# A post-norm decoder layer on one core: the order of steps on five engines, and which PSUM bank each step uses

## What is computed

```python
x = layernorm(x + self_attn(x, Wqkv, q_norm_w, k_norm_w, Wo))   # 16 heads of 32, RMS norm, RoPE, window 256 >= 128 tokens
x = layernorm(x + xattn(x, ctx, ctx))    # q, k, v taken as [8 heads, 16, 512]: scores are 512 x 512 per head, softmax, times v
x = layernorm(x + quant_dequant(x) @ quant_dequant(weight).T)   # blocks of 128, float8_e4m3
```

## Time and profile before

| | before |
|---|---|
| three timed runs, us | 3165.31, 3169.12, 3169.35 (median 3169.12) |
| the profiled execution, us | 3158.94, span 3157.2 |
| mean granted TensorE clock | 0.991 |
| PE busy | 2997.6 us, 95% of the span |
| DVE / ACT / POOL busy | 77% / 65% / 55% |

### The profile page before, as it was taken

How to read it: one execution, slowest core, us unless ns; L and a number is a source line. 1 busy time by engine, 2 the same in 40 slices (tenths; PEclk the granted TensorE clock), 3 DMA queues, 4 the chain that set the end, 5 groups by cost and what they waited for, 6 DMA issues and landing times.

```text
span 3157.2 us, 81086 instructions
## 1 busy us (share of the span) xinstructions
PE 2997.6 (95%) x22032; PEld 1545.2 (49%) x22032; DVE 2438.6 (77%) x3843; ACT 2062.5 (65%) x3713; POOL 1721.5 (55%) x1880
## 2 busy tenths in 40 slices
PE   2799999999999999999999999999999999999986
PEld 1545555555555555555554554554554554555532
DVE  5477887887787888787887787887778788878773
ACT  0467676676676676666667667667667667667653
POOL 2445665555555555565565555565555555556542
PEclk9999999999999999999999999999999999999998
DMA  2133333333333333333333333333333333333231
GB/s 80 41 97 99 94 95 94 100 92 92 93 93 97 98 96 92 91 95 95 99 93 92 91 97 93 94 96 93 94 91 95 94 99 95 90 98 100 87 103 35
DMA packets 350793, 289.05 MB, mean 92 GB/s; under 512 B 119296, under 2 KB 307712, under 8 KB 350464
## 3 DMA queue, kind: packets, MB, share of 16 engines
q1 hardware_dynamic: 350464, 286.03, 29.9%
HBM read 208.68 MB, written 77.07 MB: 91 GB/s over the span
## 4 chain that ended last, share of the span: by engine, by line
PE 90%; issue 3%; DVE 3%; ACT 2%; POOL 1%; DMA 1%; ACTq 0%; POOLq 0%; SPq 0%; DVEq 0%
PE bank L907 30%; PE st L1030 16%; PE pv L1042 15%; PE mx L1016 10%; PE bank L900 5%; PE bank L942 4%; PE bank L985 2%; PE bank L968 2%; PE bank L955 2%; PE bank L988 2%; PE bank L958 2%; ACT pp L604 1%; DVE nm L753 1%; POOL qkn L541 0%; POOL ropeA L537 0%
## 5 line engine op out<-in xcount | busy, mean ns | idle before, releaser
L753 DVE TENSOR_REDUCE nm<-mx 128x2 f32<-128x1024 f32 x1024 | 1251.4, 1222 | 401.1 <-PE mx L1016 395.3
L604 ACT ACTIVATE pp<-st 128x512 f32<-128x512 f32 x2048 | 1177.8, 595 | 415.4 <-PE st L1030 375.9
L1030 PE MATMUL st<-qst,kst 98*128 98x512 f16 x2048 | 732.1, 387 | 32.9 <-ACT pp L604 29.8
L1042 PE MATMUL pv<-pp,vT 128*32 128x512 f32 x4096 | 549.1, 608 | 0.7 <-ACT pp L604 0.7
L1016 PE MATMUL mx<-kpair,qpair 64*128 64x512 bf16 x2048 | 400.3, 388 | 14.6 <-DVE nm L753 14.6
L1030 PEld LDWEIGHTS st<-qst,kst 98*128 98x128 bf16 x2048 | 179.0, 97 | 443.8 <-issue 230.5
L907 PE MATMUL bank<-w_h,xT_h 128*128 128x512 f32 x768 | 386.9, 504 | 8.4 <-DVE xT_l L784 6.5
L547 POOL TENSOR_SCALAR_AFFINE_SELECT p<-p 128x512 f32<-128x512 f32 x256 | 163.1, 637 | 423.5 <-ACT p L656 423.5
L656 ACT ACTIVATE p<-bank 128x512 f32<-128x512 f32 x256 | 152.6, 596 | 277.1 <-PE bank L968 269.7
L1016 PEld LDWEIGHTS mx<-kpair,qpair 64*128 64x128 f16 x2048 | 98.2, 92 | 458.9 <-issue 358.0
L907 PE MATMUL bank<-w_l,xT_h 128*128 128x512 f32 x768 | 305.5, 398 | 0.0
(11 more groups left out here) (128 smaller groups left out, 5166.8 us busy)
## 6 DMA issues: line engine op xcount, KB each, us to landing
qst<-q_planes SPq DMA_DIRECT2D x640, 64.0 KB, 2.2
kst<-k_planes SPq DMA_DIRECT2D x640, 64.0 KB, 2.2
kpair<-k_planes SPq DMA_DIRECT2D x1024, 32.0 KB, 1.7
qpair<-q_planes SPq DMA_DIRECT2D x1024, 32.0 KB, 1.8
k_planes<-kpl SPq DMA_DIRECT2D x64, 384.0 KB, 2.6
xb<-x SPq DMA_DIRECT2D x64, 256.0 KB, 2.6
cx<-ctx SPq DMA_DIRECT2D x64, 256.0 KB, 2.7
x_rows<-x SPq DMA_DIRECT2D x64, 256.0 KB, 2.1
```

What stands on the lines that cost most here:

```text
L604: a.activation(pp[:, unit % 2, j, :], st[n % 2][:], ACT.Exp, scale=CROSS_SCALE).then_inc(st_free, 1)
L753: v.tensor_reduce(cols, mx[:], AX.X, ALU.max, negate=True).then_inc(mx_free, 1)
L1030: t.matmul(st[n % 2][:], kst[:, h, i * P:(i + 1) * P], qst[:, h, :], start=True, stop=True).then_inc(st_full, 1)
L1042: last = t.matmul(pv[32 * j:32 * j + 2 * XD, :], vT[b.i][:, i, GH * g + j, :], pp[:, unit % 2, j, :], start=(i == 0), stop=(i == KC - 1))
```

## The change

All five step tables and the bank table are rewritten; nothing else. Each engine runs the same steps for the same batches with the same instructions; what differs is their order in the slot, the stage at which some run, and the bank of 14 of the 25 uses. The seam between two slots moves too: on TensorE the table begins with `cross_scores_T:15` where it began with `cross_scores_T:5`, and on ScalarE with `probs:9` where it began with `oT_high:0` and `probs:4`. The number of slots, the loop's start and its 26 iterations stay.

```diff
         ACT_STEPS = steps("""
-            oT_high:0@2 probs:4@4 probs:5@4 probs:6@4 probs:7@4 self_stack:3@1 probs:8@4 probs:9@4
...
+            probs:9@4 probs:10@4 context_high:0@2 probs:11@4 probs:12@4 self_stack:3@1
...
         PE_STEPS = steps("""
-            cross_scores_T:5@4 cross_pv:0@4 cross_scores:15@4 cross_scores_T:6@4
...
+            cross_scores_T:15@4 self_scores:3@1 cross_scores_T:16@4 x_T:0@0 cross_scores_T:17@4
...
         BANK = {
-            "xT": 2, "q": 2, "k": 1, "v": 2, "tqk0": 1, "tqk1": 0, "tqk2": 1, "tqk3": 0, "s1m0": 1,
...
+            "xT": 0, "q": 0, "k": 1, "v": 2, "tqk0": 1, "tqk1": 0, "tqk2": 0, "tqk3": 2, "s1m0": 2,
```

More of the change, by code:

```diff
@@ L191, in post_ln_decoder_kernel @@
         SP_STEPS = steps("""
-            st_x2:0@4 st_kpl:0@4 ld_sh1:0@3 ld_kst:0@5 st_qpl:0@4 st_sh2:0@5 ld_sh2:0@5
-            ld_kpair:0@4 ld_x2r:0@6 ld_qpair:0@4 ld_qst:1@5 ld_kst:1@5 st_out:0@7 st_sh2:1@5
-            ld_x:0@1 ld_sh2:1@5 ld_cx:0@3 ld_kpair:1@4 ld_qst:0@4 ld_qpair:1@4 st_sh1:0@2""")
+            st_x2:0@4 ld_qpair:0@4 ld_kst:1@5 ld_x2r:0@6 st_sh2:1@5 ld_cx:0@3 ld_qst:1@5
+            ld_sh2:1@5 ld_x:0@1 ld_kpair:1@4 st_out:0@7 ld_qpair:1@4 ld_qst:0@4 st_sh1:0@2
+            st_kpl:0@3 ld_kst:0@4 ld_sh1:0@2 st_qpl:0@3 st_sh2:0@4 ld_sh2:0@4 ld_kpair:0@3""")
@@ L195, in post_ln_decoder_kernel @@
         POOL_STEPS = steps("""
[L196 to L200, removed]
-        ACT_STEPS = steps("""
-            oT_high:0@2 probs:4@4 probs:5@4 probs:6@4 probs:7@4 self_stack:3@1 probs:8@4 probs:9@4
[L203 to L209, removed]
@@ L218, in post_ln_decoder_kernel @@
-        PE_STEPS = steps("""
-            cross_scores_T:5@4 cross_pv:0@4 cross_scores:15@4 cross_scores_T:6@4
[L220 to L238, removed]
@@ new lines, in post_ln_decoder_kernel @@
+            mask:1@2 rope_sum:1@1 mask:2@2 mask:3@2 part_low:1@1 oT_low:0@2 layer_rstd:2@6
+            layer_rstd:1@5 layernorm:1@5 layer_rstd:0@2 layernorm:2@6 context_rest:0@2
+            quant_unit:0@5 layernorm:0@2 context_rest:1@2 quant_round:0@5 quant_round:1@5
+            mean_square:0@0 quant_round:2@5 query_low:0@2 rope_sum:0@0 mean_square:1@0
+            part_low:0@0 mask:0@1""")
+        ACT_STEPS = steps("""
+            probs:9@4 probs:10@4 context_high:0@2 probs:11@4 probs:12@4 self_stack:3@1
+            self_stack:1@1 probs:13@4 probs:14@4 probs:15@4 probs:16@4 xT_high:0@0 probs:17@4
+            context_high:1@2 group_out:0@4 probs:18@4 probs:19@4 probs:20@4 probs:21@4
+            query_high:0@2 probs:22@4 square:0@0 probs:23@4 probs:24@4 probs:25@4 square:1@0
+            xdT_high:0@5 part_high:0@0 probs:26@4 probs:27@4 value:0@0 probs:28@4 self_probs:0@1
+            probs:29@4 probs:30@4 self_probs:1@1 probs:31@4 probs:0@3 self_probs:2@1 probs:1@3
+            self_probs:3@1 part_high:1@0 probs:2@3 probs:3@3 group_out:1@4 probs:4@3
+            self_stack:0@0 probs:5@3 self_stack:2@0 probs:6@3 oT_high:0@1 probs:7@3
+            context_out:0@2 probs:8@3""")
@@ new lines, in post_ln_decoder_kernel @@
+        DVE_STEPS = steps("""
+            cross_max:13@5 cross_max:14@5 self_recip:0@3 cross_max:15@5 self_norm:0@3
+            cross_max:0@4 cross_shift:1@5 cross_norm:1@6 cross_max:1@4 self_max:0@2 add_cross:0@6
+            cross_max:2@4 add_self:0@3 self_max:1@2 quant_scale:0@6 cross_max:3@4 self_max:2@2
+            self_max:3@2 xT_low:0@1 cross_max:4@4 quant_magic:0@6 cross_max:5@4 self_shift:0@2
+            cross_max:6@4 rope_terms:0@1 cross_max:7@4 cross_norm:0@5 cross_shift:0@4
+            cross_max:8@4 xdT_low:0@6 cross_max:9@4 rope_terms:1@1 cross_max:10@4 cross_max:11@4
+            add_ffn:0@6 cross_max:12@4""")
@@ new lines, in post_ln_decoder_kernel @@
+        PE_STEPS = steps("""
+            cross_scores_T:15@4 self_scores:3@1 cross_scores_T:16@4 x_T:0@0 cross_scores_T:17@4
+            cross_pv:3@4 cross_scores:4@3 cross_scores_T:18@4 cross_scores_T:19@4 proj_q:0@0
+            proj_q:1@0 cross_scores_T:20@4 cross_scores:5@3 cross_scores_T:21@4 proj_q:2@0
+            cross_scores_T:22@4 proj_q:3@0 cross_scores_T:23@4 proj_k:0@0 cross_scores:6@3
+            cross_pv:4@4 cross_pv:5@4 cross_scores:7@3 cross_scores_T:24@4 cross_scores_T:25@4
+            group_T:0@4 quant_T:0@5 proj_k:1@0 proj_k:2@0 proj_k:3@0 cross_scores:8@3
+            cross_scores_T:26@4 proj_v:0@0 proj_v:1@0 cross_scores:9@3 cross_scores_T:27@4
+            proj_v:2@0 proj_v:3@0 cross_scores_T:28@4 ffn:0@5 cross_scores:10@3
+            cross_scores_T:29@4 self_scores_T:0@1 ffn:1@5 ffn:2@5 cross_scores:11@3
+            cross_scores_T:30@4 ffn:3@5 self_scores_T:1@1 self_scores_T:2@1 cross_scores_T:31@4
+            cross_scores_T:0@3 cross_scores:12@3 cross_pv:6@4 self_pv:0@1 self_pv:1@1
+            cross_scores_T:1@3 cross_scores_T:2@3 cross_scores:13@3 self_scores_T:3@1 cross_pv:7@4
+            cross_scores_T:3@3 cross_scores:14@3 self_pv:2@1 self_pv:3@1 cross_scores_T:4@3
+            parts_T:0@0 cross_scores_T:5@3 cross_scores:15@3 parts_T:2@0 cross_scores_T:6@3
+            cross_pv:0@3 cross_scores:0@2 cross_scores_T:7@3 context_T:0@2 self_scores:0@0
+            group_T:1@4 cross_scores_T:8@3 cross_scores:1@2 cross_pv:1@3 cross_scores_T:9@3
+            back_T:0@4 proj_o:0@1 proj_o:1@1 cross_scores:2@2 cross_scores_T:10@3 proj_o:2@1
+            proj_o:3@1 cross_scores_T:11@3 cross_scores_T:12@3 parts_T:3@0 parts_T:1@0
+            cross_scores_T:13@3 self_scores:1@0 cross_pv:2@3 cross_scores:3@2 cross_scores_T:14@3
+            self_scores:2@0""")
```

7 lines of the change are left out of this document (removed), and 4 rows, old and new, of the table BANK.

## The result

The changed kernel takes 3220.72 us (median of 4 runs, 3191.02 to 3225.03), the kernel before in the same comparison 3169.23: a ratio of 1.0145 [1.0084, 1.0207]. It is slower by 1.5%, where 3064 us was forecast. The profiled execution took 3221.95 us, its span is 3220.2.

A forecast was written before the change was run, and what follows sets the result against it. TensorE was taken to bound the kernel; 62 us from layout changes less new waits, 41.6 from ScalarE's seam and 2 from the ramps, 105.6 in all, bring 3169.12 to 3063.5, predicted as 3064 us, range 3044 to 3108.

The forecast's parts named there:

- What bounds the kernel: TensorE, busy for 95% of the span; only its own turns or its waits can move the time by much.
- The rival's 3213 us for a slower case: SyncE's `ld_qpair:0` comes late for an earlier pair, so every batch waits 2.5 us a slot; 3213 us, chance 0.03.
- Layout changes: TensorE's array layout changes go from 48 to 40 a slot, saving 1.08 us a slot, 64 us over 59 slots.
- Two PV units side by side: New TensorE adjacency, taken at 0.88 us start to start, as from a PV unit to a self PV unit.
- The 0.14 for projection parts behind short transposes: Cost a slot on TensorE where three parts now follow short transposes or `self_scores_T`; bounds 0 to 0.27 us.
- ScalarE's seam: ScalarE's loop return keeps its 2.79 us gap, but TensorE no longer waits for it; the whole 41.6 us go.
- the cover: TensorE work between `cross_scores_T:8` and `:11`, over 4.4 us, hides the 3.87 us until `probs:9` is seen.
- New waits: TensorE waits brought by the new order: 0.03 us a slot taken, bounds 0 and 0.3.
- three thin places: Next to no slack at `cross_scores_T:15` behind two `self_stack` copies, `self_scores:2`, and pair 0 after pair 15.
- Bank turns: no term: Readers of the banks (copies, maxima, rope terms) come a few steps ahead of the next use, so no cost.
- the rival with 0.5 us a slot: New waits at the thin places, mainly behind the two copies, cost 28 us, so 3092 us; chance 0.12.
- The ramps: First and last slots: work moved from the last into the first saves 2 us, bounds 8 either way.

The follow-up runs named there:

- the moved kernel: Changed kernel with 128 more already fulfilled wait instructions at TensorE's start, ahead of its loop: 3089.98 us, ratio 0.9765.
- N = 128: Changed kernel with 128 more wait instructions ahead of TensorE's loop, order and banks the same: 3089.98 us, ratio 0.9765.
- The one run on a single adjacency: Kernel before with `quant_T:0` and `cross_pv:4` exchanged on TensorE, so a PV unit follows the pair: 3169.07 us, ratio 1.0005.
- The return put earlier: Changed kernel with 128 more waits ahead of TensorE's loop, and ScalarE's table cut ahead of `probs:5`: 3111.55 us, ratio 0.9816.
- N = 240: Changed kernel with 240 more wait instructions ahead of TensorE's loop: 3096.63 us, ratio 0.9766.
- N = 6: Changed kernel with 6 more wait instructions ahead of TensorE's loop: 3291.45 us, ratio 1.0381.
- the lengthened old loop at 36 in: Kernel before with 8 more instructions per TensorE loop pass and 194 ahead, reaching 36 instructions into an eighth block: 3172.71 us, 1.0016.

## Why the prediction was wrong

**What bounds the kernel: the step that failed.** "Nothing but TensorE's own turns, or a wait of TensorE, can move this time" took TensorE's instructions as always at hand. The loop's return was looked at on ScalarE, VectorE and SyncE, never on TensorE. The page did show q8 with 39 blocks for 49,000 instructions run, few enough that the loop's code cannot have been fetched again at each return; that this could end was not asked. The sum has no term for it, no rival named it, and it is worth 126 us in the profiled execution: 3220.2 - 126 = 3094, near the 3088.0 us of the moved kernel's span. The rival's 3213 us for a slower case was near the time by chance; its cause, late `ld_qpair`, was not seen.

The Trainium skill ("Runtime: NRT & Kernel Launch", Instruction fetch mechanics) gives TensorE 128 KiB for instructions, filled in blocks of 16 KiB ahead of the program counter, and a fetch to wait for when a branch's target is outside the window of blocks it holds. The traces agree: nine blocks of 16,384 bytes are fetched for each stalled return, which fits eight held. It was read for ScalarE only; for TensorE, 1572 instructions against 2048 looks safe, and the runs show that it isn't when the loop reaches far enough into an eighth block (19 to 29 instructions here).

**Layout changes: right in direction, a little small.** 1.08 us a slot was forecast. The first slot of the changed kernel without waits takes 44.78 us against 46.09: 1.30 less. Two PV units side by side are 0.86 us start to start, where 0.88 was taken. The 0.14 for projection parts behind short transposes holds: with N = 128 the first matmul of such a part is 0.32 us from its second (1211.97 to 1212.29), against 0.23 for the next, and the transposes ahead of it are 0.03 shorter than elsewhere, which makes some 0.05 at each of three places. Where the other 0.2 us come from no run takes apart. The one run on a single adjacency confirmed its own 0.2 us locally and nothing of it in the time.

**ScalarE's seam: right.** The gap is still there 25 times ("ACT pp L605 <- issue", 52.3 us), and passes without a stall of TensorE show nothing of it: with N = 128 its slots are 45.4 and 45.5 us in turn, one with the return and one without. The return put earlier confirms the cover.

**New waits: mis-sized.** 0.03 us a slot was taken, 0.69 is there (45.47 - 44.78). None of the three thin places is in it. Most stands before `quant_T`, whose bank VectorE's `rope_terms` of q frees late (ropeB, L797), and the rest before `back_T`, behind `cross_norm` (yq, L838). "Bank turns: no term" was the error; the size is near that of the rival with 0.5 us a slot, whose reason (the two copies) it was not. Moving the two steps brought back 0.49 and 0.13: slots of 44.85 in the mean.

**The ramps: mis-sized.** 2 us less was taken. In spans, the start of slot 5 comes at 247.3 us instead of 222.4, and from slot 64's start to TensorE's last matmul it is 155.4 us instead of 165.7: 15 us more in all. No run here takes that apart.

**The account**, profiled spans, before to changed: slots 5 to 63 lose 59 x 1.30 = 77 us by layout and 42 by the seam, gain 59 x 0.69 = 41 by new waits and 126 by stalls, together 48 (2761.5 to 2809.8 measured); the ramps add 15; 3157.2 to 3220.2. Without the stalls the forecast would have been 3064 against 3090, inside its range.

**What stays open.** Whether the time in the eighth block is what decides the race. The table above sorts by it, but a run that keeps the place and only slows or speeds the loop's last instructions was not made. In the same bracket of time the changed kernel stalls in 16, 22 or 24 returns, and its executions differ among themselves, so something else has a part. Why ScalarE's fetch ended when its loop was cut elsewhere is open too.

## What to carry to other kernels

When an unrolled loop on the engine that bounds the kernel nears the size of its instruction store, read the instruction queue's block count before and after each edit, and compare the first matmuls behind the branch; a few no-op waits ahead of the loop tell code placement from order in one run. Place the loop (or shorten it) so that it stays in seven blocks of 256 before an ordering change is judged. An engine's loop return that does cost a fetch should stand where the waiting engine has work for longer than the gap: put earlier, the same gap cost 21.6 us (3089.98 to 3111.55). But look first whether the gap has to be there: another cut of ScalarE's table ended it altogether, worth 1.4% here.

## What was not expected of the hardware

- One code fetch at the wrong moment costs a TensorE loop of 1572 instructions nine blocks and 7.9 us: two stalls of 2.8 and 2.1 us in the mean, then about 4 us at the 1.2 GHz level (granted clock 0.67 in 1232 to 1238 us) although matmuls ran without a gap.
- 22 instructions more or less ahead of a loop change this kernel's time by 6% (3096.63 us with N = 240, which is 16 short of a whole block, to 3291.45 with N = 6).
- ScalarE's return costs 2.5 to 2.9 us from branch to next instruction at one cut of its table and 0.26 us at another, with the same 312 instructions in a pass.
- The share of returns that stall varies between executions: 3191.02 to 3225.03 us for the changed kernel, 3161.91 to 3204.68 for the lengthened old loop at 36 in, where the kernel before stays within 0.8% in every comparison.
